# Graph network kernel: column table moved to SBUF, adjacency products of a step evicted at once, out-degrees summed per step

## The reference

```python
x = _layernorm(x + L0(x))   # segment_sum((x @ W)[src] * (edge_attr @ edge_w), dst) + b
x = _layernorm(x + L1(x))   # (segment_sum(x[src], dst) / max(in_deg, 1)) @ W_l.T + b_l + x @ W_r.T
x = _layernorm(x + L2(x))   # segment_sum(x[src] * rsqrt(out_deg)[src] * rsqrt(in_deg)[dst], dst) @ weight + bias
x = _layernorm(x + L3(x))   # gated: z = tanh(norm. sum of (x @ gcn_w)[src]), g = sigmoid(z @ gate_w ..), batch norm
```

## Time and profile before

| | us |
|---|---|
| median of 3 runs (lowest, highest) | 3571.62 (3569.56, 3572.81) |
| the profiled execution | 3552.04 |
| its span, first to last instruction | 3550.3 |
| PE busy | 2287.1 (64%) |
| DVE busy | 1600.3 (45%) |
| ACT busy | 498.3 (14%) |
| POOL busy | 1616.9 (46%) |
| mean granted TensorE clock | 0.741 of full speed |

### The profile page before, as it was taken

One profiled execution on the slowest core, in us unless ns is written; L12 is line 12 of the kernel. 1 busy time (PEld: TensorE's weight loads), 2 busy tenths in 40 slices (PEclk: granted clock), 3 DMA queues, 4 the chain that ended last, 5 costly groups with the idle time before them and its releaser, 6 DMA issues.

```text
span 3550.3 us, 35883 instructions
## 1 busy us (share of the span) xinstructions
PE 2287.1 (64%) x13014; PEld 1443.9 (41%) x13014; DVE 1600.3 (45%) x2521; ACT 498.3 (14%) x761; POOL 1616.9 (46%) x1695
## 2 busy tenths in 40 slices
PE   3365556665665566656566566566678699879970
PEld 2243334443443344334344344344444344545540
DVE  3255545555545545455545555454563411321136
ACT  0011111111111111111111111111110300201113
POOL 6665656656656655566555565555540200000000
PEclk6556666666667677777776777777789899889995
DMA  5122223323333333334343434343449677627641
GB/s 181 51 82 83 83 86 85 98 80 100 97 94 94 97 103 99 110 96 118 96 115 107 129 112 122 107 129 105 131 120 203 234 290 290 260 84 290 272 145 36
DMA packets 405652, 462.56 MB, mean 130 GB/s; under 512 B 160261, under 2 KB 298986, under 8 KB 405242
## 3 DMA queue, kind: packets, MB, share of 16 engines
q1 hardware_dynamic: 184686, 284.42, 22.9%
q0 software_dynamic: 54480, 112.65, 11.7%
q10 hardware_dynamic: 166332, 63.48, 7.3%
HBM read 372.09 MB, written 88.32 MB: 130 GB/s over the span
## 4 chain that ended last, share of the span: by engine, by line
another core or an unknown queue 38%; PE 35%; issue 9%; DVE 9%; ACT 5%; DMA 1%; POOL 1%; ACTq 1%; DVEq 1%; SPq 0%; POOLq 0%
PE pb L1384 7%; PE pb L1385 7%; PE pb L1251 5%; ACT tmp L1450 4%; PE pb L1224 4%; PE pb L1214 3%; PE pb L1172 3%; PE pb L1230 2%; PE pb L1283 2%; DVE big L769 2%; DVE big L767 1%; PE pb L1359 1%; DVE big L734 1%; PE pb L1393 1%
## 5 line engine op out<-in xcount | busy, mean ns | idle before, releaser
L675 POOL DMA_INDIRECT big<-xw,big x1612 | 1523.0, 945 | 1035.0 <-issue 534.2
L838 DVE TENSOR_TENSOR big<-pb,big 128x512 f32<-128x512 f32 x404 | 259.6, 684 | 1146.4 <-remote 835.4
L1224 PE MATMUL pb<-big 128*128 128x98 f16 x3136 | 272.0, 247 | 769.3 <-ACT tmp L1450 637.0
L1251 PEld LDWEIGHTS pb<-big 128*128 128x128 f32 x3232 | 519.4, 245 | 376.7 <-issue 368.0
L1251 PE MATMUL pb<-big 128*128 128x64 f32 x3232 | 559.1, 333 | 154.1 <-issue 139.2
L1450 ACT CAST tmp<-pb 128x784 f16<-128x784 f32 x392 | 318.3, 812 | 2116.0 <-remote 1564.1
L1224 PEld LDWEIGHTS pb<-big 128*128 128x128 f16 x3136 | 229.9, 123 | 846.3 <-issue 396.8
L1384 PE MATMUL pb<-big,yT 128*128 128x512 f16 (+1 forms) x1274 | 460.2, 369 | 31.6 <-DVE yT L1047 28.1
L1385 PE MATMUL pb<-big,yT 128*128 128x512 f16 (+1 forms) x1274 | 460.1, 369 | 0.0
L767 DVE TENSOR_TENSOR big<-pb,big 128x2048 f16<-128x2048 f32 x196 | 447.2, 2282 | 0.8
L1172 PE MATMUL pb<-big 64*128 64x512 f32 x808 | 316.6, 870 | 110.3 <-DVE big L838 82.9
(11 more groups left out here) (191 smaller groups left out, 1407.7 us busy)
## 6 DMA issues: line engine op xcount, KB each, us to landing
big<-at SPq DMA_DIRECT2D x24, 6272.0 KB, 17.9
at<-tmp SPq DMA_DIRECT2D x196, 392.0 KB
big<-at ACTq DMA_DIRECT2D x32, 896.0 KB
big<-xw,big POOLq DMA_INDIRECT x1612
big<-in_ea SPq DMA_DIRECT2D x202, 64.0 KB
big<-at SPq DMA_DIRECT2D x13, 896.0 KB
big<-at ACTq DMA_DIRECT2D x24, 336.0 KB
tmp<-at ACTq DMA_DIRECT2D x8, 896.0 KB
```

What stands on the lines that cost most here:

```text
L675: nc.gpsimd.indirect_dma_start(gath[:, T8 * (n % NG) + t % T8, :], None, xw_d, bass.IndirectOffsetOnAxis(ap=src_i[:, t:t + 1], axis=0)).th ...
L838: nc.vector.tensor_tensor(msg[:, T8 * (n % 2) + 4 * q:T8 * (n % 2) + 4 * q + 4, :], PB[:, q, :].rearrange("p (t f) -> p t f", f=D), gath[: ...
L1224: last = nc.tensor.matmul(PB[:, 4 + g, i * KW:i * KW + KW], hot_lo[:, at_pair, :], hot_key[:, at_pair, :], start=True, stop=True)
L1251: last = nc.tensor.matmul(PB[:, 2 + n % 2, 0:WIN], msg[:, T8 * (n % 2) + t, :], hot_win[:, T8 * (n % 2) + t, :], start=(t == 0), stop=(t = ...
```

## The change

- `cols` becomes an SBUF tensor of 16-bit floats; `window_hot` compares with `cols_pf`, 32-bit columns in SBUF. Banks 6 and 7 are free for products.
- `a_products(j)` issues all 16 pairs of a slice ahead of the wait for the messages, four to each of banks 4 to 7, with one increment of `s_amm`. In the free columns of bank 4 a second set of 16 matmuls with the same operands sums the slice's one-hot products, which is the slice's share of the out-degrees.
- ACT evicts the four banks with one instruction, and the 98 sums with another into `sdeg_in`; one increment of `s_aev`. It now also waits until DVE has added `sdeg_in` of two slices back.
- DVE adds `sdeg_in` to `sdeg_sum` once per slice, in the step after the products. The matmuls of `out_degrees` are gone, and with them the reduction over 392 columns at the end, which reads 98 now.
- In step 5 DVE also clamps each entry of `win_tab` from below, 15 more instructions of one row, and the window addition of the first fold's step waits for them.

```diff
-        cols = PB[:, 7, 0:P + KW]
+        cols = sb("cols", [P, P + KW], F16)
+        sdeg_in = sb("sdeg_in", [P, 2, KW])
+        sdeg_sum = sb("sdeg_sum", [P, KW])
...
-                nc.vector.tensor_tensor(hot_win[:, at_tile:at_tile + T8, :], cols[:, 0:WIN].unsqueeze(1).broadcast_to([P, T8, WIN]),
+                nc.vector.tensor_tensor(hot_win[:, at_tile:at_tile + T8, :], cols_pf[:, 0:WIN].unsqueeze(1).broadcast_to([P, T8, WIN]),
...
-                    v.wait_ge(s_amm, 2 * (j - HS + 1))
+                    v.wait_ge(s_amm, j - HS + 1)
...
+                if n == STEP_OF[0]:
+                    v.wait_ge(s_off, 1)
...
+            def out_degrees(j):
+                v.wait_ge(s_aev, j + 1)
+                if j == 0:
+                    nc.vector.tensor_copy(sdeg_sum[:, :], sdeg_in[:, 0, :]).then_inc(s_sd, 1)
+                else:
+                    v.wait_ge(s_sd, j)
+                    nc.vector.tensor_tensor(sdeg_sum[:, :], sdeg_sum[:, :], sdeg_in[:, j % 2, :], ALU.add).then_inc(s_sd, 1)
...
+                if 0 <= n - 1 - LAG < NA:
+                    out_degrees(n - 1 - LAG)
...
+                        here = win_tab[0:1, STEP_OF[g]:STEP_OF[g + 1] if g + 1 < NG1 else NH]
+                        last = nc.vector.tensor_scalar(here, here, float(GB * P * (g + 1)), None, ALU.max)
...
-            def a_products(j, half):
-                if half == 0:
-                    pe.wait_ge(s_hot, j + 1)
-                if 2 * j + half > 0:
-                    pe.wait_ge(s_aev, 2 * j + half)
-                for g in (0, 1):
-                    for i in range(GP):
-                        at_pair = NPR * (j % HS) + 2 * GP * half + GP * g + i
-                        last = nc.tensor.matmul(PB[:, 4 + g, i * KW:i * KW + KW], hot_lo[:, at_pair, :], hot_key[:, at_pair, :], start=True, stop=True)
+            def a_products(j):
+                pe.wait_ge(s_hot, j + 1)
+                if j > 0:
+                    pe.wait_ge(s_aev, j)
+                pairs = [NPR * (j % HS) + i for i in range(NPR)]
+                for i, pair in enumerate(pairs):
+                    at_col = i % GP * KW
+                    nc.tensor.matmul(PB[:, 4 + i // GP, at_col:at_col + KW], hot_lo[:, pair, :], hot_key[:, pair, :], start=True, stop=True)
+                    if i >= GP:
+                        nc.tensor.matmul(PB[:, 4, AW:AW + KW], hot_lo[:, pair, :], hot_key[:, pair, :], start=(i == GP), stop=False)
+                for i, pair in enumerate(pairs[0:GP]):
+                    last = nc.tensor.matmul(PB[:, 4, AW:AW + KW], hot_lo[:, pair, :], hot_key[:, pair, :], start=False, stop=(i == GP - 1))
                 last.then_inc(s_amm, 1)
...
-                if 0 <= n - LAG < NA:
-                    a_products(n - LAG, 1)
-                if 0 <= n - LAG - 1 < NA:
-                    out_degrees(n - LAG - 1)
...
+                    act.wait_ge(s_sd, j - 1)
+                act.wait_ge(s_amm, j + 1)
+                nc.scalar.copy(stage[:, j % 2, :].rearrange("p (h d) -> p h d", d=SN).rearrange("p h (k i a) -> p h k i a", k=GA, a=2),
+                               PB[:, 4:8, 0:AW].rearrange("p k (i h a) -> p h k i a", i=GP, a=2))
+                nc.scalar.copy(sdeg_in[:, j % 2, :], PB[:, 4, AW:AW + KW]).then_inc(s_aev, 1)
```

More of the change, by code:

```diff
@@ L478, in general_dve @@
                     v.wait_ge(s_pe, NH + 1)
-                    v.wait_ge(s_amm, 2 * NA)
+                    v.wait_ge(s_amm, NA)
                 else:
@@ L567, in _ @@
                 if 0 <= j < NA:
-                    sp.wait_ge(s_aev, 2 * (j + 1))
+                    sp.wait_ge(s_aev, j + 1)
                     sp.dma_start(at_d[j], stage[:, j % 2, :]).then_inc(s_ast[j % 2], 16)
@@ L583, in _ @@
             sp.wait_ge(s_add, NH)
-            sp.wait_ge(s_amm, 2 * NA)
+            sp.wait_ge(s_amm, NA)
             sp.wait_ge(s_lk, NPB)
@@ L852, in _ @@
                     for g in range(NG1):
-                        last = nc.vector.tensor_scalar(flags[:, 3 + g:4 + g], half_i[:, STEP_OF[g]:STEP_OF[g] + 1], float(GB * P * (g + 1)), None, ALU.is_lt)
+                        nc.vector.tensor_scalar(flags[:, 3 + g:4 + g], half_i[:, STEP_OF[g]:STEP_OF[g] + 1], float(GB * P * (g + 1)), None, ALU.is_lt)
+                        here = win_tab[0:1, STEP_OF[g]:STEP_OF[g + 1] if g + 1 < NG1 else NH]
+                        last = nc.vector.tensor_scalar(here, here, float(GB * P * (g + 1)), None, ALU.max)
                     last.then_inc(s_off, 1)
@@ L893, in _ @@
             nc.vector.tensor_scalar(on_f[:, :], off_f[:, :], -1.0, 1.0, ALU.mult, ALU.add).then_inc(s_off, 1)
-            v.wait_ge(s_sd, 1)
-            nc.vector.tensor_reduce(out=fast_deg[:, 0, :], in_=PB[:, 6, 0:NB * T8].rearrange("p (h d) -> p h d", d=T8), axis=AX.X, op=ALU.add).then_inc(s_off, 1)
+            v.wait_ge(s_sd, NA)
+            nc.vector.tensor_reduce(out=fast_deg[:, 0, :], in_=sdeg_sum[:, :].rearrange("p (h a) -> p h a", a=2), axis=AX.X, op=ALU.add).then_inc(s_off, 1)
             v.wait_ge(s_lact, 3)
@@ L1214, in job @@
                             nc.tensor.matmul(bank, parts_v[part_of][:, b0 + b, :], a_piece[:, :, b, :], start=(b == 0 and part_of == 0), stop=(b == size - 1 and part_of == 1))
-            def a_products(j, half):
-                if half == 0:
-                    pe.wait_ge(s_hot, j + 1)
-                if 2 * j + half > 0:
-                    pe.wait_ge(s_aev, 2 * j + half)
-                for g in (0, 1):
-                    for i in range(GP):
-                        at_pair = NPR * (j % HS) + 2 * GP * half + GP * g + i
-                        last = nc.tensor.matmul(PB[:, 4 + g, i * KW:i * KW + KW], hot_lo[:, at_pair, :], hot_key[:, at_pair, :], start=True, stop=True)
-                last.then_inc(s_amm, 1)
[L1227 to L1233, removed]
+            def a_products(j):
[10 more added lines that the diff above has]
+                    last = nc.tensor.matmul(PB[:, 4, AW:AW + KW], hot_lo[:, pair, :], hot_key[:, pair, :], start=False, stop=(i == GP - 1))
+                last.then_inc(s_amm, 1)
             pe.wait_ge(s_rowev, 2 * NT)
@@ L1239, in _ @@
                 if 0 <= n - LAG < NA:
-                    a_products(n - LAG, 0)
+                    a_products(n - LAG)
                 pe.wait_ge(s_msg, 2 * n + 2)
@@ L1267, in _ @@
             pe.wait_ge(s_hot, NA)
+            pe.wait_ge(s_aev, NA)
             nc.tensor.matmul(PB[:, 7, 0:3 + NG1], ones[:, :], flags[:, :], start=True, stop=True).then_inc(s_off, 1)
@@ L1297, in _ @@
             pe.wait_ge(s_msg, 2 * NH)
-            pe.wait_ge(s_aev, 2 * NA)
             first_pieces = -(-(LB - DONE[NCK - 1]) // JB)
@@ L1446, in evict @@
                     act.wait_ge(s_ast[j % 2], 16 * (j // 2))
-                for half in range(2):
-                    act.wait_ge(s_amm, 2 * j + half + 1)
-                    c = half * 4 * GP
-                    nc.scalar.copy(stage[:, j % 2, :].rearrange("p (h d) -> p h d", d=SN)[:, :, c:c + 4 * GP].rearrange("p h (k i a) -> p h k i a", k=2, a=2),
-                                   PB[:, 4:6, 0:AW].rearrange("p k (i h a) -> p h k i a", i=GP, a=2)).then_inc(s_aev, 1)
+                    act.wait_ge(s_sd, j - 1)
[3 more added lines that the diff above has]
+                nc.scalar.copy(sdeg_in[:, j % 2, :], PB[:, 4, AW:AW + KW]).then_inc(s_aev, 1)
             def piece_in(i, c, b, size):
```

## The result

The changed kernel takes **3426.84 us** (median of 4 runs, 3414.97 to 3441.06) beside 3572.22 us (3569.56 to 3573.68) for the kernel before: ratio **0.960, 95% interval 0.958 to 0.963**. The profiled execution took 3414.97 us, its span is 3413.3 us, against 3552.0 and 3550.3.

What follows compares the result with a forecast made beforehand. POOL's indirect gathers were taken as the nearest bound of the edge loop: 1976 us plus 414 for the table plus some 10 of pauses, against 2540, gives 140 us less, 3432 us. Range 3280 to 3690.

Steps and rivals of the forecast that it cites:

- The total: Whole kernel: POOL's 2390 us plus some 10 of pauses against 2540, 140 us less, 3432 us; this case had 0.60.
- What bounds the kernel: Edge loop: POOL nearest the bound, 1976 us of gathers; 564 us standing still, nearly all waiting for DVE's message product.
- One PE update and one eviction: Adjacency products: two held releases in series per step become one; POOL's pauses, at most 564 us, go but for the first.
- the first rival: The rival Pauses stay: POOL still waits for the messages on top of the table's 414 us; 3704 us, chance 0.13.
- The column table in SBUF: DVE's one-hot instructions: both inputs in SBUF make POOL's gathers late, 2.11 us a step, 414 us; bounds 1.4 and 3.35.
- no seam: Rival: POOL shut out from L767's start to L769's end (the large one-hot instructions), 657 us; 3665 us, chance 0.13.
- Table instructions at twice the rate: Rival: 16-bit operands cut L767 and L769 to 1.21 and 0.96 us, price 118 us; 3226 us, chance 0.05.
- Small terms: Out-degree matmuls (+0.2 us of PE a step), ACT's evictions, DVE's addition (0.25 us a step) and clamps: nothing in the time.
- Pauses stay: Rival: DVE still falls four steps behind; with half the 564 us of pauses left, 132 us slower, 3704 us; chance 0.13.
- The forecast of faster: Whole kernel: chance 0.68 that the change makes it faster, against 0.06 same and 0.26 slower.

Runs made afterwards that it cites:

- all but the table: Changed kernel with the column table back in PSUM bank 7 and the products of each step's last four pairs left out; 3644.4 us, ratio 1.009, chip K.
- the table alone: Kernel before with only the column table moved to SBUF, both updates and evictions kept; 3441.47 us, ratio 0.951, chip K.
- the kernel with four memsets: Kernel before with four small GpSimd memsets after the fourth gather of each step; 3120.20 us, ratio 1.043 (chip M); 3123.63 us, 1.044 (chip N).
- the memsets: Kernel before, table in PSUM, with eight small GpSimd memsets after the fourth gather of each step; 3469.91 us, ratio 0.959, chip L.

## Why the prediction was right, and where it was wrong

**The total.** 12.06 us a step forecast, 12.08 measured; 140 us off the loop, 135 measured; 3432 us, 3426.84 measured. The terms were 42 us too high for the gathers (414, 372 measured) and 21 too low for the pauses (10, 31.4 measured), which in part cancel.

**What bounds the kernel**: right. POOL's gathers are the nearest bound, at 1976 us of the loop, and the 564 us beside it are pauses from held updates. Chip M shows it from the other side: without holds the kernel before takes 580 us less.

**One PE update and one eviction**: this step failed, although its result (the pauses gone but for the first) came true. I argued that halving the number of held releases in series takes the pauses away. The kernel with all but the table has the halved chain and pauses of 616.6 us; the kernel with the table alone has the full chain and 81.4. What took the pauses away was the long gathers, the term that I had booked as cost only. That the pauses went where the sum needed it was luck, as far as this step goes. The evidence stood in two places of my own text: the earlier trace rows show updates coming through when the gathers pause, and the first rival names, as an argument against itself, that each L767 now makes a pause of 1 to 2 us. I let that stand as a side remark and gave the effect to the part of the diff that looked like the purpose. Had I put the two together, the table would have been a cost and a gain at once, and the sum the same. What the halved chain is worth of itself stays open: 31.4 us of waits with it, 81.4 without, on different chips.

**The column table in SBUF**: right in mechanism, a little high. 414 us forecast, 1895.0 - 1523.0 = 372 measured, 1.90 us a step in place of 2.11, well over the lower bound of 1.4; 358 on chip M. The seam held, so *no seam* (3665) is out. By the Trainium skill's inference (SBUF — State Buffer, "Who interferes with whom") the gathers' price would have been 0; they went from 945 to 1176 ns, and the trace does not agree.

**Table instructions at twice the rate**: out. With all operands 16 bits wide L769 takes 2285 ns and L771 1781, as with the PSUM operand. The unit-step condition of the Trainium skill (Vector Engine (DVE) Microarchitecture Reference, 5.1) fits this; no run here has every operand at unit step to test it.

**Small terms.** The eviction of 1568 columns took 1.466 us (bounds 0.81 and 1.62), the copy 0.247, DVE's addition 0.251 (forecast 0.25); the sixteen degree products cost nothing that could be measured, on chip M.

**Pauses stay**: out on the chip of the forecast, where 31.4 us of them are left. Chip M shows a case that I had not considered, since I took the holds in one trace for a property of every chip: there the full cost of the table is paid and there is nothing to win. On N, where only the kernel with four memsets ran, nothing is held either. The forecast of faster is true of the chip it was made for; the changed kernel was timed on one chip more, and there it is false.

## What to carry to other kernels

Where a queue of indirect gathers runs without a break, look for instructions that finish early and are noticed late; one to two microseconds a step taken out of the stream can be worth more than they cost. Before giving a gain to the part of a diff that looks like its purpose, run that part alone and everything but that part. And a gain that comes from how a chip delivers its signals has to be timed on several chips: here the same change is 4% faster on one chip and 12% slower on another, and the untouched kernel is the best on the second. And when an experiment gives the time that a theory asks for, look whether its trace shows the theory's mechanism too: the memsets gave the time, but their breaks let no more updates through than an ordinary gather.

## What the runs showed of the hardware

- On the chip of the rows, K and L, PE's updates reach the others late while POOL's indirect gathers stream (16.92 us in the earlier trace rows, 3.7 us in the mean of the kernel before), and mostly come through when POOL stands still (95% of those pending); with SP's direct loads in their place (2317 us) none is late. On chips M and N there is no such delay (0.11 us to ACT's start in the changed kernel on M), and the kernel before takes 2992 and 2992 us against 3609 and 3617.
- A gather that starts inside a DVE instruction with two SBUF inputs ends 0.82 us after it, 2.38 in place of 0.94 us beside L769, and this price is there on both kinds of chip (372 us in all, 358 on M).
- The same comparison by 32 instructions with a scalar operand each, all in SBUF, left the gathers at 959 ns, but took DVE 1103 us in place of 797.
- Idle work on the busiest engine made a kernel faster: 329 us of it gave 4%.
- No version that beats both kernels on both kinds of chip was found. The table alone did best where updates are held (0.951; the changed kernel's 0.960, and its fewer microseconds, are from another chip, so their order is not certain), the kernel before where they are not.
